# A graph attention layer: which engine marks the adjacency, and the order of the work around it

## The reference, cut to what matters

```python
hs = layer_norm(x) * ln1_scale + ln1_bias          # 2048 source nodes, 256 features
ht = layer_norm(h_target) * ln1_scale + ln1_bias   # 2048 target nodes
q = (ht @ Wq + bq) / sqrt(32); k = hs @ Wk + bk; v = hs @ Wv + bv      # 8 heads of 32
logits = where(adj != 0, q @ k.T per head, -1e30)  # adj: 2048 x 2048 int32
ctx = softmax(logits) @ v
ht = layer_norm(ht + ctx @ Wo + bo) * ln2_scale + ln2_bias
y = ht + gelu(ht @ W1) @ W2
out = layernorm(x + y)
```

## Time and profile before

| | |
|---|---|
| median of three runs | 301.69 us (300.43 to 301.76) |
| the profiled execution | 301.85 us, its span from first to last instruction 300.1 us |
| busy share of the span | TensorE 77%, VectorE 74%, GpSimd 63%, ScalarE 55% |
| mean granted TensorE clock | 0.894 of full speed |
| first gather | at 89.25 us of the span |
| DMA | 58.03 MB, mean 193 GB/s over the span; 367 GB/s from 5 to 86 us |
| adjacency tiles | issued from 3.3 to 48.4 us |

### The profile page before, as it was taken

The page is one execution under the profiler, slowest core; times in us unless marked ns, Lnnn a source line. Parts: engine busy times, 40 slices in busy tenths (PEclk is TensorE's granted clock), DMA queues, the critical chain, the costliest instruction groups (busy, mean ns, idle before and its releaser), DMA issues.

```text
span 300.1 us, 4168 instructions
## 1 busy us (share of the span) xinstructions
PE 232.4 (77%) x1319; PEld 180.4 (60%) x1319; DVE 223.0 (74%) x625; ACT 166.1 (55%) x286; POOL 189.1 (63%) x203
## 2 busy tenths in 40 slices
PE   6499977762020779699798997997969999598990
PEld 6343432210010449599697796996968898487990
DVE  2579799879881687469597696899999988779111
ACT  1557899950001348668586688785666534443320
POOL 8685821168017748868878868878787687047452
PEclk9779999797555569799999999999999999869998
DMA  6999999999955544655556564546654446111110
GB/s 165 367 396 419 417 405 371 373 348 299 341 199 163 159 126 120 180 166 157 142 161 175 164 185 114 151 145 177 198 151 121 126 144 146 27 52 41 49 70 26
DMA packets 23457, 58.03 MB, mean 193 GB/s; under 512 B 4019, under 2 KB 12485, under 8 KB 21382
## 3 DMA queue, kind: packets, MB, share of 16 engines
q0 software_dynamic: 8368, 27.01, 31.4%
q1 hardware_dynamic: 14228, 29.91, 27.2%
q10 hardware_dynamic: 834, 0.79, 1.1%
HBM read 51.40 MB, written 10.49 MB: 206 GB/s over the span
## 4 chain that ended last, share of the span: by engine, by line
PE 26%; POOL 25%; DVE 16%; issue 12%; DMA 10%; ACT 9%; SPq 1%; POOLq 0%; ACTq 0%; DVEq 0%
POOL arena L757 16%; PE bank L1006 7%; DMA tab_scratch<-in_x_dram 6%; PE score L997 5%; PE bank L867 5%; POOL tab L747 4%; POOL rstd_late L777 3%; DVE arena L1697 3%; DMA arena<-kv_scratch,places 3%; DVE arena L1703 2%; ACT arena L1202 2%; ACT query L1210 2%; PE bank L975 2%; ACT arena L1193 2%; DMA tab<-in_x_dram 2%
## 5 line engine op out<-in xcount | busy, mean ns | idle before, releaser
L757 POOL DMA_INDIRECT arena<-kv_scratch,places x79 | 88.2, 1117 | 22.2 <-issue 22.2
L1006 PE MATMUL bank<-w_sb,gelu_t 128*128 128x256 f32 x256 | 63.3, 393 | 0.0
L997 PE MATMUL score<-h_t,w_sb 128*128 128x128 f32 x512 | 62.9, 277 | 0.0
L997 PEld LDWEIGHTS score<-h_t,w_sb 128*128 128x128 f32 x512 | 60.7, 194 | 0.6 <-ACT h_t L1328 0.3
L1006 PEld LDWEIGHTS bank<-w_sb,gelu_t 128*128 128x128 f32 x256 | 49.1, 199 | 6.3
L777 POOL TENSOR_TENSOR rstd_late<-var_late,minus_half 128x1 f32<-128x1 f32 (+3 forms) x23 | 21.1, 919 | 23.0 <-DVE var_late L1766 22.8
L1274 ACT ACTIVATE gelu_t<-score 128x512 f32<-128x512 f32 x32 | 19.1, 597 | 27.1 <-PE score L997 27.0
L867 PE MATMUL bank<-tab,arena 128*128 128x512 f32 x64 | 31.6, 646 | 0.5 <-DVE arena L1480 0.4
L747 POOL DMA_INDIRECT tab<-tab_scratch,places x16 | 17.7, 1109 | 19.3 <-DVE place_value L1625 15.0
L1656 DVE TENSOR_TENSOR arena<-arena,query 128x1024 f32<-128x1024 f32 (+3 forms) x22 | 24.5, 1113 | 4.7 <-DMA arena<-kv_scratch,places 2.8
L1281 ACT ACTIVATE tab<-tab,shift_late,rstd_late 128x256 f32<-128x256 f32 x16 | 9.4, 599 | 30.7 <-DVE shift_late L1796 30.7
(11 more groups left out here) (153 smaller groups left out, 427.0 us busy)
## 6 DMA issues: line engine op xcount, KB each, us to landing
arena<-in_adj_dram SPq DMA_DIRECT2D x6, 1024.0 KB, 11.9
w_sb<-in_adj_dram SPq DMA_DIRECT2D x6, 1024.0 KB, 12.9
kv_scratch<-arena SPq DMA_DIRECT2D x8, 512.0 KB, 10.0
tab<-in_x_dram SPq DMA_DIRECT2D x4, 512.0 KB, 10.9
own_t<-in_adj_dram SPq DMA_DIRECT2D x2, 1024.0 KB, 14.7
gelu_t<-in_adj_dram SPq DMA_DIRECT2D x2, 1024.0 KB, 11.8
tab_scratch<-in_L_gnn_h_target_dram SPq DMA_DIRECT2D x1, 2048.0 KB, 12.3
tab_scratch<-in_x_dram SPq DMA_DIRECT2D x1, 2048.0 KB, 16.7
```

Of the source, the lines that this page charges most:

```text
L757: pool.indirect_dma_start(kv_ring[:, ring_at[m] + j, :], None, kv_dram[:, :], at).then_inc(gathered[m][piece], 16)
L997: mm = pe.matmul(hid_ps[(2 * n + half) % 3][:, f % 4 * P:(f % 4 + 1) * P], w1_sb[:, k, f * P:(f + 1) * P], h2_t[:, n % 2, k, :], start=(k ...
L1006: pe.matmul(ff_ps[:, 0:D], gelu_t[:, n % 2, f, :], w2_sb[:, f, :], start=(f == 0), stop=False, skip_group_check=True)
```

## The change

- `COMPARED` is gone. ScalarE marks and sums all 16 tiles with `find_edges`; `compare` and `count` and their semaphores are gone. Loads and keys wait for `edges_ready` alone.
- GpSimd: each set of four V additions waits for the first picked bank of its quarter (the last set: for the third quarter's split); the constants wait for the first quarter's split, the bias splitting for the second's, and comes ahead of V additions 8 to 15.
- TensorE, VectorE and ScalarE: `project`, `add_bias` and `pick_bank` are called tile by tile and bank by bank in a new order. The fourth quarter's keys come ahead of the mean, which now waits for all picks.
- SyncE: the two bias loads are issued ahead of adjacency tile 4, not behind tile 11.

```diff
-    COMPARED = [0, 1, 2, 3, 10, 14]
...
+        PER_LIST = 2 + UB + 1 + 3 * UB
         def edges_free(eng, t):
             if t >= ER:
                 eng.wait_ge(coded, QK * (t // QT - ER // QT + 1))
-            if t - ER in COMPARED:
-                eng.wait_ge(counted, COMPARED.index(t - ER) + 1)
         def wait_marked(eng, t):
-            compared = sum(o <= t for o in COMPARED)
-            eng.wait_ge(edges_ready, t + 1 - compared)
-            if compared:
-                eng.wait_ge(edges_compared, compared)
+            eng.wait_ge(edges_ready, t + 1)
...
# GpSimd
             def add_v(c):
+                if c < QUARTERS - 1:
+                    pool.wait_ge(keys_read, QK * c + 1)
+                else:
+                    wait_listing(c - 1)
...
+            def wait_listing(q):
+                pool.wait_ge(pick_step, PER_LIST * q + 3 + UB)
...
             add_v(0)
+            wait_listing(0)
             pool.memset(below[:, :], 1.0).then_inc(const_step, 1)
...
             add_v(1)
-            add_v(2)
-            add_v(3)
+            wait_listing(1)
             pool.memset(bias_rows[:, :], 0.0).then_inc(bias_step, 1)
...
             pool.sem_inc(bias_ready, 1)
+            add_v(2)
+            add_v(3)
...
# TensorE: make_keys loses a wait, project_mean waits for the last picks
-                    if q == QUARTERS - 1 and n == QK - 1:
-                        pe.wait_ge(mean_copied, 1)
...
-                pe.wait_ge(keys_read, QK * (QUARTERS - 1))
+                pe.wait_ge(keys_read, QK * QUARTERS)
```

## The result

Measured: 292.24 us, median of 4 runs (290.82 to 294.01), against 301.73 for the kernel before beside it: ratio 0.970 (0.9645 to 0.9751), 9.5 us less. The forecast was 296.6 (294.2 to 300.5): faster as said, by nearly twice as much, and under the range. The profiled execution took 292.31 (span 290.6; before 301.85, 300.1). Medians and ratios from here on leave out runs that fell into a slower state, more than 1.5% above the fastest of the same kernel.

The account below looks back on a forecast made before the run. VectorE was taken to bound the front before the first gather; the front's 5.9 us less 0.8 for the gather meeting weight loads gave 5.1 us off 301.85, or 296.6 us against the runs' median, range 294.2 to 300.5.

Parts of the forecast that it names:

- Who bounds the front, and by how much: Before the first gather: VectorE ends the front; six comparisons, 6.8 us of work, leave it; front 5.9 us earlier.
- The walk: VectorE's front, operation by operation at start-to-start prices: slot table at 82.5, with 0.6 for handoffs 83.1, against 88.95.
- GpSimd's place: GpSimd work beside VectorE's key splitting: splits 0, 1 and 3 clean, split 2 charged 0.8 us, copies staying at 0.95.
- The floor: Copy of x into tab_scratch, needed by the first gather: lands at 81.8 less about 0.4; gain 7.2 us at most.
- rival (1): Front: handoffs cost nothing, split 2 clean, table ready at 81.7 together with the copy of x; 294.9 us; chance 0.12.
- The first gather under weight loads: First own-row gather meets Wo, W1 and W2 still in the queue: charged 0.8 us, bounds 0 and 3.5.
- I take it to shift as a whole: Everything behind the first gather at 89.25, 211 us, keeps its length and only starts earlier.
- A: Follow-up theory, behind the first gather: the shortening there was the clock's pattern in these executions; filled kernels 6.6 us apart.
- B: Follow-up theory, behind the first gather: the change itself shortens that part; filled kernels 8.5 us or more apart.
- (3): ScalarE's marks held by three turned-chunk copies waiting 3.03 us each: 8.6 us late, 305.2 us; chance 0.08.
- (4): Behind 89: gathers meet the weights at the upper bound and the mean row lands late; 300.6 us; chance 0.10.
- Rival (2): TensorE's clock falls to half under projections 13 to 15: 301.1 us, for one of them 298.4; chance 0.14.

Follow-up runs that it names:

- marks_only: Kernel before with ScalarE marking all tiles and SyncE's loads in the new order; TensorE, VectorE and GpSimd orders as before: 295.73 us, ratio 0.984.
- pool_old: Changed kernel with GpSimd's order and waits of the kernel before: 294.59 us, ratio 0.981.
- again: Changed kernel unchanged, run again on another chip: 292.72 us against 299.37 for the kernel before, ratio 0.980.
- delay2: Changed kernel with two unused chained comparisons on VectorE ahead of the slot table: 297.84 us, ratio 0.994.
- after: First profiled execution of the changed kernel: 292.31 us, against 301.85 for the kernel before.
- delay: Changed kernel with six unused chained comparisons on VectorE ahead of the slot table: 301.69 us against 300.45 for the kernel before, ratio 1.004.
- again2: Changed kernel unchanged, in a later run: 294.46 us against 300.98 for the kernel before, ratio 0.9755.
- late_sums: Changed kernel with V additions 8 to 11 waiting for the end of the third split: 293.37 us, ratio 0.980.
- filled pair: Changed kernel and kernel before, both with idle TensorE transposes ahead of its waits at groups 1, 9 and 13: 292.39 and 299.38 us.
- lead_warm: Changed kernel with idle TensorE transposes between the last keys and first own rows and inside the lead: 294.36 us, ratio 0.984.

## Why the prediction was too cautious

- **Who bounds the front, and by how much**: right. marks_only shows the removed comparisons, with ScalarE's and SyncE's new order, to be worth 5.0 us; the marks on ScalarE cost its end nothing (57.3; forecast 57.5).
- **The walk**: keys 1 at 40.4 (measured 40.31), keys 2 at 49.8 (49.70), bias 13 at 54.6 (54.47), bias 15 at 57.7 (57.76), keys 3 57.8 (57.55), picks 3 64.6 (64.45), list end 72.5 (72.32), table 82.5 (82.34). The 0.6 us "for handoffs" had no row behind it, and nothing came for it. With 0.2 of drift it is the first miss: 0.7. From the first picks to the table the walk gives 51.2 us, and two profiles measured 51.25. That its start fitted so well (31.3) is in part luck: the first picks of the changed kernel began at 31.09, 30.93, 32.02 and 31.63 in its four profiles, by the clock of the first 20 us, and the first gather at 82.48 to 83.58.
- **GpSimd's place**: right in kind. Split 2 cost 0.93 over a clean one (0.8), the copies 0.71 (0.95); pool_old gives 0.6 us for the whole edit. Which operation pays varies: across V additions 8 to 11 the cast at 58.42 took its 0.22, and the operations behind it 0.64 and 1.15 (0.23 and 0.63 in the last split); in pool_old, beside the splitting of the biases, the last split's cast took 0.56. MAX8 took 0.87 everywhere. The rule of the Trainium skill ("SBUF — State Buffer", Who interferes with whom), by which a VectorE operation in a two-port mode and a GpSimd operation exclude each other, fits this in kind; no row names the mode. The prediction's bound of 1.54 us was itself taken from the 3.33, so that the 3.33 agrees with it was no test; 0.93 came.
- **The floor** at 81.4 to 81.8 was a wrong bound: I held landings to follow only the bytes in the queue. The copy of x was issued at 60.59 and landed at 78.0, 3.8 us earlier than before, when issued 4.4 earlier (in again it landed at 79.6). It didn't decide here, but rival (1) stood on it.
- **The first gather under weight loads**: charged 0.8, measured 0 (3.55 us to landing, 3.7 before). The second miss: 0.8, and part of it is the luck of this execution: in later profiles of the changed kernel and its variants the landing took 3.6 to 5.6, so the bounds 0 to 3.5 were fair, and the "under 1 us" was once exceeded. The mean row, sent at 69.37 (69.3), cost nothing: the first K/V gather followed the first gather by 1.56 us, as before.
- **The step that failed: "I take it to shift as a whole".** A shift does pass through (delay2). But the 210.9 us of the profile of before are one draw: with the second part's instructions unchanged, profiles gave 207.8 (again), 208.0 (after), 208.9 (pool_old), 209.0 (delay), 209.1 (again2), 210.2 (delay2) and 211.2 (late_sums). After drew a short one: 2.9 us, which the sum had put at nothing. The front's gain alone would have given 295.1, inside the range. Sum: 0.7 + 0.8 + 2.9 = 4.4 = 9.5 - 5.1.
- A against B: the filled pair (7.0) and again2 (6.5) favour A. The three comparisons on undisturbed chips gave 9.5, 6.65 and 6.5 us, so a lasting gain of about 7 is what is shown, some 2.5 of the first result's 9.5 were luck, and up to 1 us of B isn't excluded. Whether the clock falls after a given wait looks like chance per execution; what decides it stays open.
- Rivals (3) and (4) did not occur: added waiting on ScalarE 0.75 us in all, nothing eaten behind 82. Rival (2) did not in this run (granted clock 1.00 from 56.10 to 59.50); its mechanism did in delay2 and lead_warm, at 25 to 30 us.

## What to carry to other kernels

Walk the critical engine instruction by instruction with start-to-start prices and trust it: from the first picks to the table it was within 0.1 us over 51, and an allowance without a row only biases it. Its starting point has a spread, here 1.1 us with TensorE's clock of the first 20 us, and two profiles that differ by less say nothing until that point is taken off. A stretch that "just shifts" has its own spread too: here 3.4 us from shortest to longest, where TensorE's clock falls after short waits, and the range needs it on both sides. Before explaining a few us behind a change, run the unchanged kernel again elsewhere, and fill the idle waits in both kernels.

## What the hardware showed unexpectedly

- A wait of TensorE of 2.0 to 3.2 us was followed, in some executions, by 3.4 or 6.8 us at half clock, priced at 1.3 to 1.9 us of total time; a full clock through the whole lead gained nothing in the median (294.36 against 292.72).
- The clock's first stretch at half, 6.8 us long, lay at 10.4 or at 12.7 us in executions of one kernel, and moved everything up to the first gather by 0.9 us.
- Two of the chips ran every version 4 to 9 us slower (before: 306.38 and 308.82 against 299.37 to 301.73), with waits put down to `remote` in the profile; why is open.
